# Row fetches of the relation layer turned round: one-hots stationary, row parts moving, no transposes

## The reference, cut to what matters

```
x1 = layernorm(x + L0(x))
coef = w_comp[etype]                         # one of 32 relations, 8 bases
msg  = sum over b of (x1[src] @ weight[b]) * coef[:, b] * norm
out  = layernorm(x1 + relu(segment_sum(msg, dst) + bias))
```

## Time and profile before

| | us |
|---|---|
| median of 3 runs | 3584.79 (3584.2 to 3587.19) |
| the profiled execution | 3587.32 |
| its span, first to last instruction | 3585.6 |
| first node gather of the relation stage | 2145.2 |
| first tile sum of step 0 | 2159.05 |
| last fetch matmul | 3462.7 |
| last node gather | 3560.8 |

### The profile page before, as it was taken

How to read it: one execution, slowest core, us unless ns; L and a number is a source line. 1 busy time by engine, 2 the same in 40 slices (tenths; PEclk the granted TensorE clock), 3 DMA queues, 4 the chain that set the end, 5 groups by cost and what they waited for, 6 DMA issues and landing times.

```text
span 3585.6 us, 53206 instructions
## 1 busy us (share of the span) xinstructions
PE 3287.7 (92%) x17323; PEld 2222.0 (62%) x17323; DVE 2449.7 (68%) x4752; ACT 1343.9 (37%) x3346; POOL 2355.0 (66%) x2636
## 2 busy tenths in 40 slices
PE   3999999998998989999998979999999999999984
PEld 2889999997553333354343436767667766676764
DVE  7999999997777656510210327888778888778772
ACT  5999999997000000000100113333333333333320
POOL 5888888885004777744545407777767777677775
PEclk6999999999999999999999989999999999999995
DMA  6677777777877999999999953333333333333332
GB/s 185 190 206 206 207 207 206 209 206 234 292 256 230 242 228 242 251 270 261 267 260 262 278 184 82 83 83 86 82 83 85 85 84 86 79 86 85 84 76 55
DMA packets 537244, 616.88 MB, mean 172 GB/s; under 512 B 79129, under 2 KB 465401, under 8 KB 536841
## 3 DMA queue, kind: packets, MB, share of 16 engines
q1 hardware_dynamic: 483335, 530.00, 53.3%
q0 software_dynamic: 53632, 83.43, 9.5%
HBM read 443.98 MB, written 169.24 MB: 171 GB/s over the span
## 4 chain that ended last, share of the span: by engine, by line
PE 54%; ACT 19%; DMA 14%; DVE 7%; issue 3%; POOL 3%; DVEq 0%; POOLq 0%; SPq 0%
PE PS L1248 18%; PE PS L1300 14%; DMA arena<-adjacency 13%; ACT arena L864 12%; PE PS L1343 7%; ACT arena L880 6%; PE PS L1326 5%; PE PS L1362 2%; POOL arena L816 2%; PE PS L1136 2%; PE PS L1287 1%; PE PS L1335 1%; DVE H L1793 1%; DVE arena L1719 1%; DVE arena L1457 1%
## 5 line engine op out<-in xcount | busy, mean ns | idle before, releaser
L816 POOL DMA_INDIRECT arena<-x_table,rec x1088 | 1038.5, 954 | 400.3 <-issue 302.4
L794 POOL DMA_INDIRECT sorted_records<-arena x480 | 567.1, 1181 | 564.0 <-PE PS L1248 462.5
L1136 PE MATMUL PS<-arena 128*98 128x128 f32 x6272 | 761.7, 279 | 45.5 <-ACT arena L880 12.1
L1136 PEld LDWEIGHTS PS<-arena 128*98 128x98 f32 x6272 | 708.6, 166 | 94.9 <-issue 50.4
L751 POOL TENSOR_SCALAR arena<-iota,H,arena 128x98 f32<-128x98 f32 x980 | 674.1, 701 | 91.9 <-PE PS L1136 89.4
L1248 PE MATMUL PS<-arena,X 128*128 128x512 f32 (+1 forms) x1274 | 547.9, 580 | 65.2 <-DMA arena<-adjacency 64.8
L864 ACT ACTIVATE arena<-arena 128x98 f32<-128x98 f32 x1568 | 582.6, 686 | 11.6 <-DVE arena L1537 11.6
L1248 PE MATMUL PS<-arena,H 128*128 128x512 f32 (+1 forms) x1274 | 537.9, 575 | 41.4 <-DMA arena<-adjacency 40.5
L1300 PE MATMUL PS<-H,X 128*128 128x512 bf16 x1764 | 526.5, 380 | 19.3 <-DVE H L1793 19.3
L880 ACT ACTIVATE arena<-PS 98x1024 f32<-98x1024 f32 x392 | 519.3, 1325 | 12.7 <-PE PS L1136 12.7
L1719 DVE TENSOR_TENSOR arena<-arena 128x1536 f32<-128x1536 f32 (+1 forms) x192 | 344.1, 1792 | 188.3 <-DMA arena<-adjacency 183.3
(11 more groups left out here) (263 smaller groups left out, 2937.0 us busy)
## 6 DMA issues: line engine op xcount, KB each, us to landing
arena<-adjacency SPq DMA_DIRECT2D x294, 768.0 KB, 8.6
adjacency<-arena SPq DMA_DIRECT2D x196, 784.0 KB
arena<-adjacency SPq DMA_DIRECT2D x98, 832.0 KB, 6.3
arena<-x_table,rec POOLq DMA_INDIRECT x1088
arena<-in_edge_type SPq DMA_DIRECT2D x540, 32.0 KB
XT<-sorted_source_rows SPq DMA_DIRECT2D x126, 128.0 KB
XT<-sorted_relations SPq DMA_DIRECT2D x504, 8.0 KB
sorted_records<-arena POOLq DMA_INDIRECT x480, 7.4
```

The lines of the kernel that those rows point to most:

```text
L794: pool.indirect_dma_start(rec2_d, bass.IndirectOffsetOnAxis(ap=SLOT[:, t:t + 1], axis=0), R4[:, t, :], None).then_inc(s_scat, 16)
L816: pool.indirect_dma_start(G[:, step % HELD_STEPS * STEP_TILES + j, :], None, x1_d, bass.IndirectOffsetOnAxis(ap=SRC[:, t:t + 1], axis=0)). ...
L1136: last = nc.tensor.matmul(bank(2 * q + j // 4, P, j % 4 * P)[0:M1, :], S1[:, r, :], S2[:, r, :], start=True, stop=True)
```

## The change

The roles in the row fetch are exchanged. A piece is now one tile c of the group: for each block j the one-hot of this tile, ST2[:, j, 128 columns], is stationary, and the 128 columns of each of the three row parts are moving. So a piece is 21 matmuls of 128 columns into 128 columns of bank 2, and there are four pieces in a step. The result has edges in the partitions at once. The transposes, the copy GT, `turned_copied` and the semaphore s_turned go; ScalarE's one copy writes G2 directly, and waits for the wide sums of two groups before. The wide sums wait for s_gc. UNITS has no "turn" entry.

```diff
-            def sources(i, j):
+            def sources(i, c):
                 first = group_of(i) // ROUNDS_SORTED * CLASS_BLOCKS
-                if j == 0:
+                if c == 0:
                     pe.wait_ge(s_st2, i + 1)
                     if i:
                         pe.wait_ge(s_gc, i)
-                if i < CLASSES:
-                    pe.wait_ge(s_low, CHUNK_OF[first + j] + 1)
-                for a, rows_part in enumerate((XS[:, first + j, 0, :], XS[:, first + j, 1, :], LOW[:, first + j, :])):
-                    last = nc.tensor.matmul(bank(2), rows_part, ST2[i % 2][:, j, :],
-                                            start=(j == 0 and a == 0), stop=(j == CLASS_BLOCKS - 1 and a == 2))
-                if j == CLASS_BLOCKS - 1:
+                for j in range(CLASS_BLOCKS):
+                    if c == 0 and i < CLASSES:
+                        pe.wait_ge(s_low, CHUNK_OF[first + j] + 1)
+                    for a, rows_part in enumerate((XS[:, first + j, 0, :], XS[:, first + j, 1, :], LOW[:, first + j, :])):
+                        last = nc.tensor.matmul(bank(2, D, c * D), ST2[i % 2][:, j, c * P:(c + 1) * P], rows_part,
+                                                start=(j == 0 and a == 0), stop=(j == CLASS_BLOCKS - 1 and a == 2))
+                if c == PER - 1:
                     last.then_inc(s_gs, 1)
...
             def sources_copied(i):
                 act.wait_ge(s_gs, i + 1)
                 if i >= 2:
-                    act.wait_ge(s_u, UNIT[i - 2, "turn", 0] + 1)
-                nc.scalar.activation(GT[i % 2], bank(2), ACT.Copy).then_inc(s_gc, 1)
...
                     act.wait_ge(s_u, UNIT[i - 2, "wide", PER - 1] + 1)
-                nc.scalar.activation(G2[i % 2].rearrange("p t c -> p (t c)"), bank(UNIT_BANKS[n % RING_BANKS]), ACT.Copy).then_inc(s_turned, 1)
+                nc.scalar.activation(G2[i % 2].rearrange("p t c -> p (t c)"), bank(2), ACT.Copy).then_inc(s_gc, 1)
...
             def wide_summed(i, c):
                 n = UNIT[i, "wide", c]
                 unit_bank_free(n)
-                pe.wait_ge(s_turned, i + 1)
+                pe.wait_ge(s_gc, i + 1)
```

```diff
                 if ahead:
                     sources(s + 2, 0)
-                if s + 1 < GROUPS:
-                    sources_turned(s + 1)
-                if ahead:
-                    sources(s + 2, 1)
                 if s < GROUPS:
                     wide_summed(s, 0)
                     wide_summed(s, 1)
                 if ahead:
-                    sources(s + 2, 2)
+                    sources(s + 2, 1)
                 if s + 2 < STEPS:
                     coefficients(s + 2)
-                if ahead:
-                    sources(s + 2, 3)
                 for n in events_in(s - 1):
                     block_multiplied(n)
                 if s < GROUPS:
                     wide_summed(s, 2)
                     wide_summed(s, 3)
                 if ahead:
-                    sources(s + 2, 4)
+                    sources(s + 2, 2)
                 if s < STEPS:
                     tiles_summed(s, 1)
                 if ahead:
-                    sources(s + 2, 5)
-                    sources(s + 2, 6)
+                    sources(s + 2, 3)
```

More of the change, by code:

```diff
@@ L168 @@
 for step in range(STEPS):
-    if step == 0:
-        UNITS.append((0, "turn", 0))
     UNITS.append((step, "tile", 0))
-    if step + 1 < GROUPS:
-        UNITS.append((step + 1, "turn", 0))
     if step < GROUPS:
@@ L340, in regular @@
         ST2 = [h1_flat[:, j * HALF_ST2:(j + 1) * HALF_ST2].bitcast(BF16).rearrange("p (k e) -> p k e", e=PER * P) for j in range(2)]
-        GT = [unused[:, j * 512:(j + 1) * 512] for j in range(2)]
         G2 = [cut(17280 + j * PER * D, PER * D).rearrange("p (t c) -> p t c", c=D) for j in range(2)]
@@ L469, in regular @@
         s_u = sem("basis_sums_made")
-        s_turned = sem("sources_turned_copied")
         s_bp = sem("blocks_multiplied")
@@ L1057, in _ @@
             sources_copied(0)
-            turned_copied(0)
             relations(2)
@@ L1063, in _ @@
                     halved(KEPT_CHUNK + s)
-                if s + 1 < GROUPS:
-                    turned_copied(s + 1)
                 if s + 3 < STEPS:
@@ L1312, in unit_bank_free @@
                         pe.wait_ge(s_adds, added_wide(step, i))
-                    elif kind == "turn":
-                        pe.wait_ge(s_turned, step + 1)
                     else:
@@ L1328, in tiles_summed @@
                 last.then_inc(s_u, 1)
[L1330 to L1336, removed]
             def wide_summed(i, c):
@@ L1380, in _ @@
             for i in range(2):
[L1381 to L1384, removed]
+                for c in range(PER):
+                    sources(i, c)
             pe.wait_ge(s_zero, 2)
```

## The result

The changed kernel takes 3603.0 us in the median, the kernel before 3584.2 on the same chips (11 runs each): ratio 1.0061, 95% interval 1.005 to 1.0073. It is slower by 0.6%, where 0.5% faster was forecast. The profiled execution took 3609.7 us against 3587.3, 22.4 more. The median lies just inside the stated range (3550 to 3605), but that is luck: the range reached so far up for matmuls of 60 ns, which did not occur.

What follows compares the result with a forecast made beforehand. TensorE was taken to pace the steps, with GpSimd taking over after 57.9 us saved. Terms -0.44 + 0.17 + 0.11 = -0.16 us over 106 steps, with the start -17.3, took 3587.3 to 3570.0, median 3567.5; range 3550 to 3605.

Steps and rivals of the forecast that it cites:

- What bounds the kernel: Relation stage: TensorE paces 124 steps at 10.51 us; GpSimd needs 9.99 us for a step's 8 gathers.
- The room: Relation stage: TensorE savings before 3463 us show at the end until 57.9 us are used up and GpSimd rules.
- Part 1 and 2: TensorE step: transposes gone, 0.44 us less; 84 fetch matmuls of 128 columns for 21 of 512, 0.17 us more.
- unhidden loads: Row fetch: loads not hidden under the matmul before, 0.083 us a pair, +1.99 us a step, 3832 us; chance 0.08.
- small addition per matmul: Row fetch: 57.1 to 58.7 ns a matmul, about 3585 us, chance 0.14; up to 62 ns, slower, chance 0.10.
- slow instructions: TensorE's instruction queue: 118 more instructions a step, about 60 more packets, 3640 us if wholly exposed; chance 0.04.
- something else: Anything else that makes it slower, such as VectorE, busy 8.2 of 9.6 us, setting more steps; chance 0.02.
- Wrong if: Profile signs: 21 matmuls over 1.23 us, f32 start over 0.15 late, one-hot waits past 25 us, idle inside a piece.
- Part 3: F32 work behind fetches: loads stick out 0.055 us at coefficients and second tiles, 0.11 together; none at wide pairs.
- Part 5: Order of fetch pieces in a step: one-hot wait and copy wait stay, bank ring looser; no cost.
- Part 6: TensorE's 18 waits for VectorE's one-hots, 19.3 us: VectorE's finish counts there, so these steps give nothing.

Runs made afterwards that it cites:

- e6: Changed kernel with the third row part (LOW) left out of the row fetch, 56 matmuls in place of 84; ratio 0.9868 to the kernel before.
- e1: Changed kernel with its 84 fetch matmuls cut in seven pieces of 12 at the kernel before's seven places; ratio 0.9981 to the kernel before.
- e3: Changed kernel with the coefficients moved ahead of fetch piece 1, which then stands before the blocks; ratio 0.9951 to the kernel before.
- e4: Changed kernel, fetch in two runs of 42: pieces 0 and 1 between coefficients and blocks, the others behind the second tiles; ratio 0.9886 to the kernel before.
- e5: Changed kernel, coefficients first, fetch in six pieces of 14, one also between the wide sums of each pair; ratio 1.0006 to the kernel before.
- e2: Kernel before, old roles and transposes kept, with fetch piece 3 moved ahead of the coefficients; ratio 1.0097 to the kernel before.
- e7: Kernel before, old roles and transposes kept, fetch pieces 0 to 3 between coefficients and blocks, 4 to 6 behind the second tiles; ratio 0.9979.
- e8: Changed kernel with all four fetch pieces in one run between coefficients and blocks; ratio 0.9881 to the kernel before.

## Why the prediction was wrong

**What bounds the kernel: right.** TensorE is the pacemaker of the 124 steps, GpSimd lies below it and takes over when TensorE is fast enough (e6), and what TensorE gains or loses before that comes out at the end: 19.0 us of the 22.4 in the changed kernel. The room was over-counted, 57.9 us for 47: the prediction took 1.249 us for every gather and put the slower ones down to waits; and of the 74.1 us that it read as waits for TensorE, the 13.7 at the wide sums are ordinary idle time. For a change of this size that did not matter.

**Part 1 and 2, transposes and fetch: right.** -0.44 as forecast; 84 matmuls at 0.056, +0.15 for +0.17. The rivals of unhidden loads (0.083) and of a small addition per matmul fell, and so did that of slow instructions: no gap stands inside a piece. So did the 81 ns of the Trainium skill (TensorE: Matmul & The Clock Gate, "Back-to-back issue gap"). Here 0.0558 us stands in four pieces a step with a load before each matmul, in line with the 55.6 ns that the Trainium skill gives in the section "Wait — 56ns, not 53.3ns?" of the same page. Of the rivals that ended slower, none with a mechanism of its own was the case; there is left the "something else", with a chance of 0.02 and VectorE as its example, and VectorE it was not. None of the four signs under "Wrong if" came up either: it became slower in a way that the prediction had not seen.

**Part 3, f32 loads in the open: right mechanism, the sum too small.** Forecast 0.11 a step, after the wait for the copy (0.06) had swallowed one of three places; measured 0.32, from which the same 0.06 goes. The coefficients have 0.06 and both halves of the tiles 0.06, but the wide sums too, 0.06, where I wrote "no extra, since their own columns cover it". They are 1.19 behind a short fetch and 1.13 behind a long one; the columns of a matmul don't cover what comes before its own start. That the 0.056 is a part of the load is still a reading of the sizes: it goes away behind fetch matmuls of 512 columns, and no run changed the load itself. And the 0.08 of a wide sum behind the coefficients was missing, because I had not noticed that the reordering makes them neighbours in ordinary steps. The step is 9.63 - 0.44 + 0.15 + 0.32 - 0.06 = 9.60; the gain of 0.16 shrank to 0.03. e1, e3, e4 and e5 gave the size by counting places, e2 gave the 0.08.

**Part 5, the order: this step failed.** It asked where the fetch pieces went with respect to the one-hots, the copy of bank 2 and the banks of the ring, and found nothing. It did not ask what stood behind the piece that was taken away: piece 3 covered ScalarE's copy of the coefficients, for which the blocks wait. The wait is in the code (`pe.wait_ge(s_coefc, ...)` in `block_multiplied`), and the chain before had the time: 0.65 us of fetch between coefficients and block. The price, per step with a block: 0.63 of standstill and of the first block matmul, less the 0.08 that the wide sums have not to pay in such a step: 0.55, in 42 steps, 23 us. e1 takes it away by the order alone, e2 makes it by the order alone, e3 takes it away by one exchange. The steps were forecast 17 us shorter and are 19 longer; of these 36, part 5 has 23 and part 3 some 14 (0.13 in 106 steps). Without the wait the change would still have gained less than forecast, as e1 shows with 0.2%.

**Part 6, VectorE: half right.** TensorE's waits for one-hots neither went away nor grew (17.0 us for 19.3). But VectorE is no fixed bound there: they vanish when the first piece comes later in the step (e4, e7, e8).

What remains open: whether the 0.056 is a part of the f32 load, why some gathers are slower than most, where e7's smaller waits come from, and why a wide sum behind the coefficients costs 0.08.

## What to carry to other kernels

When independent work is moved in an in-order queue, ask for every gap that it leaves what the instruction behind the gap waits for: filler between a producer and a consumer on the same engine is cover, even if it has nothing to do with either. Count the places where a short matmul of 16-bit operands is followed by f32 work: here each cost 0.056 us, so that one long run costs one and four pieces cost four. And before a wait in a profile is counted as room to gain, lay it beside the idle time that stands there anyway. A restructuring that saves work can lose by its order alone: here the same matmuls in other orders span from 1.0061 to 0.9881.

## What the runs showed of the hardware

A bf16 matmul of 128 columns with a new stationary tile each time goes at 0.0558 us start to start at the upper clock level (2.4 GHz), 42 in 2.35 us, with the load quite hidden. A group of f32 matmuls behind it takes 0.056 us more, whatever their columns (32, 104, 128 or 336), than behind a bf16 matmul of 512 columns (0.216). Behind f32 matmuls of 32 columns, four wide records (336 columns) take 1.21 us, 0.08 more than behind 512 bf16 columns. Behind a wait of TensorE, 16 f32 records of 128 columns take 1.86 us from start to start, without one 1.78. And an indirect gather of GpSimd is busy 0.944 us in the median but 0.954 on average, which makes 11 us in 1088 of them.
